# Last blocks of a routed layer placed by one-hot products, output bias added when a block leaves PSUM, and layer-two weights loaded early

## The reference, cut to what matters

```python
def L1_ffn(x, gate_w, w1, b1, w2, b2):      # 8 experts, the best 2 for each token
    z = layernorm(x)
    top2, weights = softmax_top2(z @ gate_w)
    for k in range(2):                       # e = expert of the token's choice k
        y[k] = gelu(z @ w1[e] + b1[e]) @ w2[e] + b2[e]
    return x + weights[0] * y[0] + weights[1] * y[1]
```

## Time and profile before

| | us |
|---|---|
| median of 3 runs | 206.13 (203.81 to 209.12) |
| the profiled execution, own time | 205.05 |
| its span, first to last instruction | 203.3 |
| PE busy | 168.1 |
| DVE busy | 125.1 |
| POOL busy | 88.6 |
| ACT busy | 83.9 |

### The profile page before, as it was taken

One profiled execution on the slowest core, in us unless ns is written; L12 is line 12 of the kernel. 1 busy time (PEld: TensorE's weight loads), 2 busy tenths in 40 slices (PEclk: granted clock), 3 DMA queues, 4 the chain that ended last, 5 costly groups with the idle time before them and its releaser, 6 DMA issues.

```text
span 203.3 us, 3874 instructions
## 1 busy us (share of the span) xinstructions
PE 168.1 (83%) x1269; PEld 148.7 (73%) x1269; DVE 125.1 (62%) x460; ACT 83.9 (41%) x225; POOL 88.6 (44%) x110
## 2 busy tenths in 40 slices
PE   1899999997978997999957999999999899796000
PEld 1336868987968896798854989999998799795000
DVE  1948889675973467767897666878653433443320
ACT  2135536523432513654213427754655466560000
POOL 4210020078757358101177873071087477711750
PEclk9999999799999999999995599999999999999555
DMA  6891000111469734541922111116233346321131
GB/s 211 269 406 40 5 0 0 52 29 39 102 150 352 199 125 95 127 102 32 297 61 53 37 44 39 53 16 78 81 65 77 56 98 70 81 63 53 52 103 52
DMA packets 13844, 19.63 MB, mean 97 GB/s; under 512 B 2162, under 2 KB 9282, under 8 KB 13826
## 3 DMA queue, kind: packets, MB, share of 16 engines
q1 hardware_dynamic: 11104, 14.00, 20.9%
q0 software_dynamic: 2432, 4.99, 14.3%
q10 hardware_dynamic: 290, 0.41, 0.5%
HBM read 14.41 MB, written 4.98 MB: 95 GB/s over the span
## 4 chain that ended last, share of the span: by engine, by line
PE 61%; DMA 13%; POOL 9%; DVE 7%; issue 5%; ACT 2%; POOLq 1%; DVEq 0%; ACTq 0%
PE bank L1596 11%; PE bank L1607 10%; DMA xg<-z_rows,idx 8%; PE bank L1563 5%; POOL xg L375 5%; PE bank L1362 4%; PE bank L1552 4%; POOL yg L389 4%; PE bank L1579 4%; PE bank L1378 3%; PE bank L1517 3%; PE bank L1337 2%; PE bank L1368 2%; PE bank L1467 2%; PE bank L1477 2%
## 5 line engine op out<-in xcount | busy, mean ns | idle before, releaser
L375 POOL DMA_INDIRECT xg<-z_rows,idx x52 | 51.8, 997 | 35.7 <-issue 14.3
L389 POOL DMA_INDIRECT yg<-y_rows,pos x24 | 23.2, 969 | 25.3 <-DMA y_rows<-PT 13.0
L360 POOL TENSOR_TENSOR rstd<-ve,neg_half 128x2 f32<-128x2 f32 (+1 forms) x14 | 10.7, 764 | 43.5 <-DVE ve L785 43.4
L593 ACT ACTIVATE hT<-bank,pb 128x128 f32<-128x128 f32 x64 | 19.2, 366 | 17.8 <-PE bank L1596 17.6
L593 ACT ACTIVATE hT<-bank,bmore 128x128 f32<-128x128 f32 x56 | 16.8, 365 | 11.2 <-PE bank L1596 11.0
L1596 PE MATMUL bank<-xT,w1s 128*128 128x128 f32 x128 | 20.5, 296 | 0.8 <-DVE xT L1046 0.5
L1596 PEld LDWEIGHTS bank<-xT,w1s 128*128 128x128 f32 x128 | 18.1, 209 | 1.7 <-DVE xT L1046 1.2
L1607 PE MATMUL bank<-w1s,hT 128*128 128x128 f32 x128 | 17.0, 276 | 0.0
L1517 PE MATMUL bank<-pa,xg 128*128 128x128 f32 x52 | 11.9, 295 | 5.9 <-DMA xg<-z_rows,idx 5.8
L1596 PE MATMUL bank<-xT,wmore 128*128 128x128 f32 x112 | 16.4, 279 | 0.1
L1033 DVE TENSOR_TENSOR hT<-sg,bank 128x512 f32<-128x512 f32 (+1 forms) x16 | 10.4, 651 | 9.3 <-PE bank L1563 7.3
(11 more groups left out here) (189 smaller groups left out, 348.0 us busy)
## 6 DMA issues: line engine op xcount, KB each, us to landing
w1s<-in_w SPq DMA_DIRECT2D x8, 512.0 KB, 6.1
w0s<-in_w SPq DMA_DIRECT2D x9, 384.0 KB, 6.3
y_rows<-keys_home SPq DMA_DIRECT2D x12, 128.0 KB, 3.2
y_rows<-PT SPq DMA_DIRECT2D x12, 128.0 KB, 1.8
xg<-z_rows,idx POOLq DMA_INDIRECT x52, 3.3
X<-in_x SPq DMA_DIRECT2D x2, 256.0 KB, 3.6
z_rows<-ZS SPq DMA_DIRECT2D x2, 256.0 KB, 2.3
rope<-in_rope_q SPq DMA_DIRECT2D x1, 512.0 KB, 4.4
```

Of the source, the lines that this page charges most:

```text
L360: nc.gpsimd.tensor_tensor(rstd[:, g, n, first:end], ve[:, g, n, first:end], neg_half[:, first:end], ALU.pow).then_inc(s["ln_rstd", g], len ...
L375: nc.gpsimd.indirect_dma_start(xg[:, g, j], None, z_rows[layer][g], bass.IndirectOffsetOnAxis(ap=idx[:, g, j:j + 1], axis=0)).then_inc(xg_ ...
L389: nc.gpsimd.indirect_dma_start(yg[:, k], None, y_rows[layer][g], bass.IndirectOffsetOnAxis(ap=pos[:, g, k:k + 1], axis=0)).then_inc(yg_in[ ...
L593: nc.scalar.activation(hT[:, i % 3, c * P:(c + 1) * P], (GATE, UP)[c // 2][:, o:o + P], ACT.Gelu, bias=bias).then_inc(s["h1_set"], 1)
```

## The change

- The last three of the 15 blocks of the last batch (12, 13, 14) no longer go through DRAM. Their 128 results each stay in SBUF. For each of the three DVE makes a table of zeros and ones (`late_rows`), which says what token each row belongs to, for choice 0 and choice 1, and PE multiplies it with the results into two banks (`late_sums`). DVE then adds both banks with the routing weights (`late_added`). The gathers of the last batch wait for six stores of pairs instead of eight; the three blocks' rows in DRAM are filled with zeros at the start.
- The output bias is added by `blocks_done`, which becomes an addition of a bias tile to the PSUM result. The bias of a further block is copied by one more DVE copy in `weights_more`. The five steps of the bias product go.
- The eight weight transfers of layer two are issued right after those of layer one.
- The rotated halves of the queries are added on DVE, and each tile has one scores product instead of two.
- `context_weights` and the making of `upper` move from DVE to POOL.
- At the start PE does 28 products of ones before the keys, the first loads are cut into smaller parts, and the first normalisation goes in halves of a batch.
- Results are gathered and added in the order choice 0, choice 1 of tile 0, then tile 1 and so on, and the output is stored in halves of a batch.
- The order of the steps on PE, ACT, DVE and POOL is written anew.

```diff
+FETCH = [k for t in range(T) for k in (t, T + t)]
+LATE = 3
+WARM = 28
...
+            sp.wait_ge(s["late_table"], 1)
+            sp.dma_start(y_rows[1][1].rearrange("(j p) d -> p j d", p=P)[:, J[1] - LATE:], no_rows
+                         ).then_inc(y_stored[1, 1], 16)
+            for e in range(E):
+                weights_in(e)
             rows_out(0, 0)
             rows_out(0, 1)
             for k in range(6):
                 blocks_out(0, 0, k)
-                if k < 2:
-                    weights_in(2 * k)
-                    weights_in(2 * k + 1)
...
-            for k in range(8):
+            for k in range((J[1] - LATE) // 2):
                 blocks_out(1, 1, k)
...
+            def late_rows(m):
+
+                dve.wait_ge(s["late_row_set"], 1)
+                if m < 2:
+                    dve.wait_ge(s["o1_psum"], 2 * B)
+                else:
+                    dve.wait_ge(s["xT_psum"], TURNS[1, 1])
+                v.tensor_scalar(late_homes[m],
+                                fetch_nos[:].rearrange("p k t q -> p (k t q)"), late_row[:, m:m + 1], None,
+                                ALU.is_equal).then_inc(s["late_hot_set"], 1)
...
+                    v.tensor_copy(b2more[:, k], b2[:, bass.ds(e, 1)].rearrange("p a d -> p (a d)"))
...
-                v.tensor_copy(ys[g][:, 2 * k:2 * k + n].rearrange("p j d -> p (j d)"),
-                              y_bank(q)[:, 0:n * P]).then_inc(s["yv_set"], 1)
...
+                v.tensor_tensor(ys[g][:, 2 * k:2 * k + n].rearrange("p j d -> p (j d)"), y_bank(q)[:, 0:n * P],
+                                bias.rearrange("p j d -> p (j d)"), ALU.add).then_inc(s["yv_set"], 1)
...
-                last.then_inc(s["q_set"], 1)
+                last.then_inc(s["q_parts"], 1)
+                dve.wait_ge(s["q_parts"], n + 1)
+                v.tensor_tensor(qr[:, 0, cols], qr[:, 0, cols], qr[:, 1, cols], ALU.add).then_inc(s["q_set"], 1)
...
+            def late_added(k):
+                dve.wait_ge(s["late_psum"], LATE)
+                dve.wait_ge(s["sc_set"], nth(1, 1))
+                for t in range(T):
+                    if k:
+                        dve.wait_ge(s["late_added"], t + 1)
+                    v.scalar_tensor_tensor(X[:, 1, t], bank[4 + k][:, t * P:(t + 1) * P], sc[:, 1, k, t:t + 1], X[:, 1, t],
+                                           ALU.mult, ALU.add).then_inc(s["late_added"], 1)
...
+            def warm_up():
+                pe.wait_ge(s["const_set"], 1)
+                for _ in range(WARM):
+                    mm(bank[5][:, 0:P], ones[:], ones[:], start=True, stop=True)
...
-                    mm(o, qr[:, 0, t * P:(t + 1) * P], keys, start=False, stop=False)
-                    last = mm(o, qr[:, 1, t * P:(t + 1) * P], keys, start=False, stop=True)
+                    last = mm(o, qr[:, 0, t * P:(t + 1) * P], keys, start=False, stop=True)
...
+            def late_sums(m):
+                q = PAIRS[1, 1] + (J[1] - LATE + m) // 2
+                pe.wait_ge(s["oh_set"], 4)
+                pe.wait_ge(s["late_hot_set"], m + 1)
+                pe.wait_ge(*y_out(q))
+                for k in range(2):
+                    if m == 0:
+                        mm(bank[4 + k][:], ones1[:], over_rows(ohb[0:1, T], T * P // E), start=True, stop=False)
+                    for t in range(T):
+                        last = mm(bank[4 + k][:, t * P:(t + 1) * P], late_hot[m][:, k, t], ys[1][:, J[1] - LATE + m],
+                                  start=False, stop=m == LATE - 1 and t == T - 1)
+                last.then_inc(s["late_psum"], 1)
```

668 lines of the change are left out of this document (346 added, 322 removed).

## The result

The changed kernel takes 195.06 us, the median of 4 runs (193.82 to 196.17). Next to it the kernel before took 207.62 (203.81 to 211.36). The ratio is 0.9515, 95% interval [0.9376, 0.9654]: faster. The ratio and its interval are taken over the faster executions of both kernels, the medians over all. I forecast 192.0, with a range from 187.0 to 198.5. The profiled execution took 194.61 us, with a span of 192.8, against 205.05 and 203.3. So the span shrank by 10.5 us where my terms sum to 13.3.

The account below looks back on a forecast made before the run. PE bounds the long middle, loads and short steps the start, the last store and eight POOL gathers the end. Terms sum to 13.3 us, from 205.05 to 191.8 or from the median to 192.8; forecast 192.0, range 187 to 198.5.

Parts of the forecast that it names:

- Start: Up to the first gather: faster and reordered key folds, earlier position product; 3.0 us gained, between 1.0 and 4.1.
- the fold "out of the way": Start: second key fold, 1.9 us, placed behind the turned rows that the first scores need, so no longer delaying them.
- Weights early: Window 55 to 66 us: 512 KB weight transfers no longer among small gathers; 2.0 us gained, at least 1.0.
- Scores: One scores product per tile instead of two, 0.32 us for each of eight tiles; 2.3 us gained, at least 1.0.
- Routing gap: Routing of layer two's batch 0: two row gathers no longer ahead of batch 1's queries; 1.4 us gained.
- The rival that PE's new head of the list waits: Routing term's bad end: batch 1's queries, now ahead of the first `up1`, wait and queue block work; 2.0 us lost.
- Turned weights: Turned weights of batch 1 in PE's full middle; 0.6 us gained, at least 0.4.
- the gap from 158 to 175 us: Batch 0's last result copied out earlier on DVE, so POOL's 2.05 us store wait goes; 2.0 us gained, at least 0.9.
- DVE and the port: Added DVE copies and tables, and gathers on POOL slowed beside them; 1.0 us charged, between 0 and 3.0.
- Tail: End of kernel: six stored pairs suffice, three blocks summed on PE and DVE; 3.0 us gained, between 3.0 lost and 3.5 gained.
- The slower case: POOL's eight new steps take 26 us and hold layer two's first gather: 212 us, chance 0.04.
- that rival: Early gains absorbed by layer two's routing waits for stores and POOL: some 5 of 7.3 us lost, 197, chance 0.14.

Follow-up runs that it names:

- g3: Changed kernel with blocks 12 to 14 of the last batch through DRAM again, without tables, late products and additions: 237.71 us, on a chip where every kernel was slower.
- f0: The changed kernel run again with no edit, as base for the edits: 194.97 us, ratio 0.9485.
- g1: Changed kernel plus twelve more products of ones on PE between the values and the first fold: 235.24 us, on a chip where the kernel before took 240.51.
- h1: Changed kernel with layer two's eight weight transfers issued among the stores of layer one again: 200.45 us, ratio 0.9796.
- f3: Changed kernel with the last two result products of layer one's batch 1 and their copies ahead of the second gate product: 194.63 us, ratio 0.9481.

## Why the prediction was right or wrong

The time lies inside the range, 3.1 us above the forecast. By stretches of the two profiles the terms did as follows; the stretches add up to the span, since each starts where the one before ends.

| stretch, its end in both traces | terms | forecast | measured |
|---|---|---|---|
| to the first row gather (41.36, 37.91) | start | 3.0 | 3.45 |
| to the turn of layer one's first block of batch 1 (67.94, 62.37) | weights | 2.0 | 2.12 |
| to the ranks of layer two's batch 0 (101.17, 97.06) | half of scores | 1.15 | -1.46 |
| to the first `down1` (122.72, 116.99) | half of scores, routing | 2.55 | 1.62 |
| to the end of the block work (184.91, 176.97) | turned weights, gap, DVE | 1.6 | 2.2 |
| to the end | tail | 3.0 | 2.5 |
| sum | | 13.3 | 10.4 |

The 176.97 is worked out: the last half of `up1` starts at 175.15, and in g3, where no `late_sums` stands between, the last product ends 1.82 later.

- **Start**, 3.0 forecast. Measured 3.45 at the first gather in one trace and 1.1 in f0. The step that failed is the fold "out of the way": the new list has it behind the turned rows but still ahead of the first scores (7.35, scores at 8.65), and without the products of ones the scores come at 12.89, as before. I gave the reordered fold most of the term and the faster fold 0.8, and the runs show the reverse. The 0.7 for the first gather is not shown either: the profile before has its clock at 0.51 from 35 to 38 us, and where the changed kernel has such a stretch (g1, g3) it takes 29.5 us from the first scores to the first gather instead of 28.1.

```profile
35.00:38.00 3.00, 3.00 (x19) 3.00 (x16) 2.72 (x15) 2.65 (x4) 0.00 (x0) 0.51 0.22 87
```

The Trainium skill ("TensorE: Matmul & The Clock Gate", What's actually happening) says that the ramp costs less than one per cent of a typical kernel and varies from run to run. The runs agree: the slow folds of f0 cost 1.76 us at its first scores, 0.9% of 195, and other executions of the same kernel don't have them.
- **Weights early**, 2.0. In that stretch 2.1. The edit undone costs 5.4, but what the gain over the kernel before is stays open: in the next stretch 1.5 us are lost again, and with late weights h1 is 3.5 slower up to the ranks than the kernel before. The price of a late weight load was read from one wait and not from the later ones.
- **Scores**, 2.3. This is the term that failed most. The forecast took 0.32 us a tile from the second product's start to the next tile; a tile got shorter by 0.22, so 0.9 a batch. And I charged all eight as if PE were full. In the stretch with batch 0's, PE's idle time grew from 2.55 to 4.22 us, with waits of 1.3 for DVE and 1.1 for gathered rows, and the stretch became longer by 1.46. The cause of these waits was not found.
- **Routing gap**, 1.4. With batch 1's scores, 1.62 of 2.55. The rival that PE's new head of the list waits did happen, and so did one of my signs of being wrong: PE idles 7.37 us between the ranks and the first `up1`, where it was 3.36. The first `up1` is only 0.39 sooner (111.58 for 111.97). It paid even so, since the queries are done by then. f3 shows part of what bounds it: POOL's chain from the last store of layer one, then DVE's row numbers.
- **Turned weights, the gap from 158 to 175 us and DVE**, 1.6 as a sum, measured 2.2. The named wait of 2.05 went, and PE's idle time in the stretch fell from 2.50 to 1.19. How the 2.2 divides over the three terms was not measured.
- **DVE and the port**. The tables took 0.73 to 0.81 us, the small copies 0.21 to 0.25. One gather of results took 1.98 while DVE made a table for 1.22, where others take 0.95; in f3, where the gather ended before that table began, it took 0.95 too. The Trainium skill's page "SBUF — State Buffer" (SBUF: two separate sides) says that a DVE step with two inputs from SBUF can lock a GpSimd step that reads SBUF out of a shared port for its whole length. The rows agree.
- **Tail**, 3.0. Measured 2.5 from the marks, 2.6 by g3. The size was near but the step was wrong: I took the products and additions for the later of two paths, at 195.7. They end 4.5 us before the span does. The span ends with POOL's DRAIN, 7.2 us after its last gather starts. The order of nine gathers, which I counted but took as covered, cost 1.25 of it.
- **POOL's new steps** took 3.4 us together, 0.31 to 0.63 each, in idle time. Three have 128 columns, four 64 and one a single one, not five wide and three narrow. The slower case is out.

The terms that fell short are the scores and what was lost beside them up to the ranks (2.6), the routing (0.9) and the tail (0.5); the start, the weights and the middle gave 1.2 more. Gains at the start are absorbed to a third, as f0 shows, and I had given that rival 0.14 as a whole and nothing as a part.

## What to carry to other kernels

Look for what ends the span: count from each engine's last instruction to the end in several traces, read the rows of the closing line too, and shorten the one whose distance is constant. Let the stretches of a forecast and of the measurement add up to the same span, so that a loss between two gains can't hide. Price a stall from an early collision at all the waits it feeds, not at the first. Take two profiles of one kernel before you explain a difference of 2 us: here the start and one wait near 77 us differed by that much with no edit, and one store near 140 with an edit that doesn't reach it.

## What the runs showed of the hardware

- POOL's closing DRAIN ended 7.2 us after its last indirect gather started, in all fourteen traces, and in eleven of them it ended the span.
- The same stretch of one program, behind a wait of PE of 1.1 to 1.4 us near 77 us, ran with the granted clock at 1.00 in one trace and at 0.50 in two others.
- The first two instructions of the fold took 1.12 or 2.08 us in two traces of one program, and none of the waits of 1.01 to 1.29 us brought the clock down where it had risen before them.
- A store of 256 KB took 2.4 us from issue to its reader in one trace and 4.3 in another.
- A DVE table of 1.22 us made a gather on POOL that ran beside it last 1.98 us instead of 0.95.
- On one chip PE, DVE and ACT stood idle together for 3 to 5 us several times, while POOL's gathers went on at 1.25 us each: PE from 189.6 to 193.1 us in g1, with no wait that the rows show. Each of five kernels took 232 to 250 us there. Why stays open.
